# Normalising x in groups of 2, 2, 4 and 2 tiles, and comparing 100 of the 157 edge columns in the loop of head pairs

## What is computed

```python
xn = _layernorm(x, axis=-1)
x = x + gnn(xn, edge_index, W, b) + mix(xn)            # graph convolution, attention
x = x + ffn(_layernorm(x))                             # 8 experts, top 1, capacity 195
# gnn: deg = count of edges by target, msg = h[row] * norm, summed by target
# mix: 12 heads; A = q @ k.T; numerator = 1 + A + 0.5 * A * A; attn = numerator / its sum; attn @ v
```

## Time and profile before

| | us |
|---|---|
| median of 3 runs | 1186.23 (1185.6 to 1189.72) |
| the profiled execution | 1186.19 |
| its span in the trace | 1184.4 |
| PE, DVE, ACT, POOL busy | 943.1, 725.0, 471.5, 308.4 |

### The profile page before, as it was taken

One profiled execution on the slowest core, in us unless ns is written; L12 is line 12 of the kernel. 1 busy time (PEld: TensorE's weight loads), 2 busy tenths in 40 slices (PEclk: granted clock), 3 DMA queues, 4 the chain that ended last, 5 costly groups with the idle time before them and its releaser, 6 DMA issues.

```text
span 1184.4 us, 15348 instructions
## 1 busy us (share of the span) xinstructions
PE 943.1 (80%) x5388; PEld 901.2 (76%) x5388; DVE 725.0 (61%) x1357; ACT 471.5 (40%) x696; POOL 308.4 (26%) x204
## 2 busy tenths in 40 slices
PE   1138747999998998998999868979999975199970
PEld 1138746898898997997988758969999975099970
DVE  6248982677767768677778835564544437056633
ACT  1211012666676676676667721210110102156620
POOL 2013345566455554454520000000000001300004
PEclk9569988999999999999999988989999985599995
DMA  8986765222524324325215055365445113769987
GB/s 232 299 279 194 186 167 107 22 37 33 89 35 65 70 33 83 62 22 100 35 22 140 27 94 144 88 158 140 118 102 142 58 53 118 230 196 266 280 221 260
DMA packets 142147, 148.33 MB, mean 125 GB/s; under 512 B 71910, under 2 KB 119497, under 8 KB 140952
## 3 DMA queue, kind: packets, MB, share of 16 engines
q1 hardware_dynamic: 112152, 125.09, 39.6%
q0 software_dynamic: 29952, 22.68, 11.6%
HBM read 93.32 MB, written 46.72 MB: 118 GB/s over the span
## 4 chain that ended last, share of the span: by engine, by line
PE 55%; DVE 16%; DMA 10%; ACT 8%; issue 7%; SPq 2%; POOL 2%; DVEq 0%; ACTq 0%; POOLq 0%
PE ps L1635 12%; PE ps L1637 11%; PE ps L1636 11%; PE ps L1019 7%; DMA kb<-keyd 4%; DVE eqs L430 4%; PE ps L1003 4%; PE ps L1004 4%; ACT Pf L711 2%; ACT Ph L683 2%; DVE Pl L867 1%; DMA rows<-oE 1%; POOL rows L1376 1%; PE ps L1269 1%; PE ps L985 1%
## 5 line engine op out<-in xcount | busy, mean ns | idle before, releaser
L356 POOL DMA_INDIRECT counts<-countc,idxu x157 | 270.4, 1722 | 288.0 <-DMA counts<-countc,idxu 230.0
L867 DVE SCALAR_TENSOR_TENSOR Pl<-Pf,Ph 125x832 fp32r<-125x832 f32 (+1 forms) x180 | 184.6, 1027 | 117.9 <-ACT Ph L683 108.9
L711 ACT ACTIVATE Pf<-ps 125x832 f32<-125x832 f32 (+1 forms) x180 | 155.7, 866 | 116.4 <-PE ps L1004 108.1
L1019 PE MATMUL ps<-Ph,vsb 125*128 125x416 f32 (+1 forms) x360 | 129.0, 358 | 6.3 <-DVE Pl L867 6.1
L1019 PE MATMUL ps<-Pl,vsb 125*128 125x416 f32 (+1 forms) x360 | 126.6, 352 | 0.0
L1376 POOL DMA_INDIRECT rows<-XF,slots x10 | 14.8, 1483 | 397.5 <-DVE slots L1491 394.8
L1635 PE MATMUL ps<-wH,XH 128*125 128x384 f32 x240 | 85.4, 356 | 20.6 <-DVE VS L469 13.6
L1635 PE MATMUL ps<-XH,wqkH 128*128 128x416 f32 (+1 forms) x216 | 81.0, 375 | 20.5 <-DVE wqkL L758 12.1
L1636 PE MATMUL ps<-wL,XH 128*125 128x384 f32 x240 | 83.5, 348 | 0.0
L1637 PE MATMUL ps<-wH,XL 128*125 128x384 f32 x240 | 83.5, 348 | 0.0
L683 ACT ACTIVATE Ph<-Pf 125x832 fp32r<-125x832 f32 (+1 forms) x90 | 80.1, 897 | 0.7
(11 more groups left out here) (229 smaller groups left out, 2224.0 us busy)
## 6 DMA issues: line engine op xcount, KB each, us to landing
Cs<-counts SPq DMA_DIRECT2D x20, 546.9 KB
kb<-keyd SPq DMA_DIRECT2D x9, 1024.0 KB, 8.1
w1s<-L_ffn_w SPq DMA_DIRECT2D x8, 1152.0 KB, 8.2
w2s<-L_ffn_w SPq DMA_DIRECT2D x8, 1152.0 KB
odram<-OHL SPq DMA_DIRECT2D x12, 625.0 KB
oS<-odram SPq DMA_DIRECT2D x10, 750.0 KB, 4.8
vdram<-VS SPq DMA_DIRECT2D x10, 672.0 KB
vsb<-vdram SPq DMA_DIRECT2D x12, 560.0 KB
```

Source lines behind the costliest of these rows:

```text
L356: pool.indirect_dma_start(out=counts, out_offset=bass.IndirectOffsetOnAxis(ap=idxu[:, c:c + 1], axis=0), in_=countc[:, c:c + 1], in_offset ...
L711: act.activation(Pf[:, i % RING, :, 0:w], ps[0:T, 2 * (i % 2):2 * (i % 2) + 2, 0:w], ACT.Square, bias=1.0).then_inc(sq_done, 1)
L867: dve.scalar_tensor_tensor(out=p, in0=f, scalar=1.0, in1=h.bitcast(F32), op0=ALU.add, op1=ALU.subtract).then_inc(p_lo, 1)
L1019: ins = pe.matmul(ps[:, 4 + s % 2, 0:w], vsb[:, 2 * kp + t, a, :], part[:, m % RING, t, 0:w], start=(kp == 0 and t == 0 and part is Ph), s ...
```

## The change

x is normalised, transposed and split in four groups of 2, 2, 4 and 2 tiles, and value tiles 0, 1 and 2 stand between them on PE, ACT and DVE. The three parts of the value weights are loaded right behind the first two tiles of x, each with a buffer of its own (the third in the upper half of `kb`). The edge lists are loaded by ACT's queue. Only columns 0 to 55 and column 156 are compared in the value stage, in seven chunks of 8 behind value tiles 3 to 9, the lone one at the end. The other 100 are compared in the loop, 20 in each of the five pairs: SP loads their keys at the head of the pair into the memory of `kt2` (`kbp`), DVE waits for them at step 3, compares one column in each of steps 4 to 23, and works out the targets in steps 24 and 25. ACT waits for `eq_over` before it writes `kt2` again. POOL fills with zeros as soon as x and the three weights are there, and scatters 57 columns, then 20 for each pair.

The diff, cut to its core:

```diff
+EARLY = 56
+EG = 8
+EU = EARLY // EG
+EP = (ET - EARLY) // 5
+LONE = ET - 1
...
-        x_in = [sem(f"x_in{i}") for i in range(NT)]
+        x_in = [sem(f"x_in{i}") for i in range(NT // 2)]
...
+        kbp = kt2[:].rearrange("p t l f -> p (t l) f")
...
+        XGROUPS = [(0, 2), (2, 2), (4, 4), (8, 2)]
+        FIRST_EDGES = 3
+        def w_staging(wc):
+            return wst[:, wc, :, :] if wc < 2 else kb[:, 1, 0:12, :].rearrange("p s f -> p (s f)").rearrange("p (k n) -> p k n", k=2)
...
                 if i == 1:
-                    sp.wait_ge(padded, 1)
-                    for h, ends in enumerate((src, dst)):
...
+                    for wc in range(3):
+                        sp.dma_start(w_staging(wc), w_parts[0][0][2 * wc * P:2 * (wc + 1) * P, :].rearrange(
+                            "(k p) n -> p k n", p=P)).then_inc(w_early[wc], 16)
...
-            load_keys(0)
-            load_keys(1)
+            load_keys(0, 0, 0, EC)
+            sp.wait_ge(w_lo, 3)
+            load_keys(1, 0, EC, EC)
...
-                if i + 2 < EU:
-                    load_keys(i + 2)
+                if i == FIRST_EDGES + 1:
+                    sp.wait_ge(eq_done, 2)
+                    load_keys(0, 0, 2 * EC, EC)
+                if i == FIRST_EDGES + 3:
+                    sp.wait_ge(eq_done, 4)
+                    load_keys(1, 0, 3 * EC, EARLY - 3 * EC)
+                    load_keys(1, EARLY - 3 * EC, LONE, 1)
...
+            normalise(0)
+            split_w(0)
+            split_w(1)
+            turned_lo(0)
+            keys_of_edges()
+            split_w(2)
+            normalise(1)
+            value_lo(0)
+            turned_lo(1)
+            normalise(2)
+            value_lo(1)
+            turned_lo(2)
+            normalise(3)
+            value_lo(2)
+            turned_lo(3)
+            for i in range(3, NT):
+                value_lo(i)
+                edge_chunk(i - FIRST_EDGES)
...
+            def load_pair_keys(j):
+
+                sp.wait_ge(g_mm, j + 1)
+                sp.dma_start(kbp.bitcast(F32), keyd[at(j * EP + EARLY, EP), :].unsqueeze(0).broadcast_to([P, EP, P])
+                             ).then_inc(keys_in, 16)
...
             def turn(j, last):
+                if not last:
+                    load_pair_keys(j)
                 sp.wait_ge(oacc_done, 6 * j + FREE)
                 load_v(j, 1)
...
                         if i - 1 in TURN_AT:
+                            if i - 1 == TURN_AT[0]:
+                                act.wait_ge(eq_over, j + 1)
                             turn_k(j + 1, TURN_AT.index(i - 1))
...
                 for i in range(END):
 
+                    if not last:
+                        if i == PAIR_KEYS_AT:
+                            dve.wait_ge(keys_in, 16 * j + 16)
+                            dve.wait_ge(idx_ready, EU + j)
+                            order(dve.tensor_scalar(kcur[:], keyc[:, at(j * EP + EARLY, EP)], 1.0, None, ALU.mult))
+                        if PAIR_KEYS_AT < i <= PAIR_KEYS_AT + EP:
+                            pair_compare(i - PAIR_KEYS_AT - 1)
+                        if i in (PAIR_TARGETS_AT, PAIR_TARGETS_AT + 1):
+                            pair_targets(i - PAIR_TARGETS_AT)
```

More of the change, by code:

```diff
@@ new lines, in value_hi @@
+            def value_hi(i):
+                for c in range(2):
+                    vg = 2 * i + c
+                    act.wait_ge(v_mm, vg + 1)
+                    if i >= 2 and c == 0:
+                        act.wait_ge(v_store[i % 2], MOVED * (i // 2))
+                    act.activation(VS[:, i % 2, 6 * c:6 * c + 6, 0, :],
+                                   ps[0:T, 4 + vg % 4, 0:HALF].rearrange("p (h f) -> p h f", h=6), ACT.Copy
+                                   ).then_inc(v_hi, 1)
@@ L439, in edge_chunk, with targets @@
+            def targets(c0, n):
+                order(dve.tensor_scalar(etmp[:, 0, 0:n], countc[:, c0:c0 + n], AGAIN, None, ALU.is_ge))
+                for h in range(min(WINDOW, n)):
+                    order(dve.tensor_scalar(etmp[:, 1, h:n:WINDOW], keyc[:, c0 + h:c0 + n:WINDOW], -1.0,
                                             iota_f[:, 10 + h:11 + h], ALU.mult, ALU.add))
                 order(dve.tensor_tensor(etmp[:, 2, 0:n], etmp[:, 0, 0:n], etmp[:, 1, 0:n], ALU.mult))
-                ins = dve.tensor_tensor(idxu[:, cs], etmp[:, 2, 0:n], keyc[:, cs], ALU.add)
@@ L442, in edge_chunk @@
-                ins.then_inc(idx_ready, 1)
+                return dve.tensor_tensor(idxu[:, c0:c0 + n], etmp[:, 2, 0:n], keyc[:, c0:c0 + n], ALU.add)
+            def edge_chunk(u):
+                first, half = u * EG, (u // 2) % 2
+                if u % 2 == 0:
+                    dve.wait_ge(kb_in[half], (16 if u < EU - 1 else 32) + 16 * (u // 4))
+                for c in range(first, first + EG):
+                    ins = compare(c, half, c % EC, WINDOW)
+                    if c % 4 == 3:
+                        order(ins)
+                if u == EU - 1:
+                    order(compare(LONE, half, EARLY % EC, 1))
+                    order(targets(LONE, 1))
+                targets(first, EG).then_inc(idx_ready, 1)
@@ new lines, in value @@
+            def value(i):
+                for c in range(2):
+                    vg = 2 * i + c
+                    if vg >= 4:
+                        pe.wait_ge(v_lo, vg - 3)
+                    product(pe, ps[0:T, 4 + vg % 4, 0:HALF],
+                            lambda k: (XH[:, k, i * T:(i + 1) * T], XL[:, k, i * T:(i + 1) * T]),
+                            lambda k: (wH[:, k, c * HALF:(c + 1) * HALF], wL[:, k, c * HALF:(c + 1) * HALF]),
+                            KT).then_inc(v_mm, 1)
@@ new lines, in _ @@
+            turn_x(0)
+            pe.wait_ge(keys, 2)
+            pe.transpose(ps[:, 7, 0:P], keyA[:], ident[:])
+            pe.transpose(ps[:, 7, P:ET], keyB[:], ident[0:ET - P, 0:ET - P])
+            pe.wait_ge(b_in, 16)
+            ins = pe.transpose(ps[:, 7, ET:ET + 3 * PAIRS], brow[:], ident[0:3 * PAIRS, 0:3 * PAIRS])
+            ins.then_inc(key_tr, 1)
+            pe.wait_ge(keyc_done, 3)
+            pe.wait_ge(w_lo, 3)
+            pe.wait_ge(xt_lo, FIRST_UNIT[1])
+            value(0)
@@ L514, in build @@
+            turn_x(1)
+            pe.wait_ge(xt_lo, FIRST_UNIT[1])
+            value(1)
+            turn_x(2)
+            pe.wait_ge(xt_lo, FIRST_UNIT[2])
+            value(2)
+            turn_x(3)
+            pe.wait_ge(xt_lo, FIRST_UNIT[3])
+            value(3)
+            for i in range(4, NT):
+                if i == 8:
+                    pe.wait_ge(xt_lo, FIRST_UNIT[4])
+                value(i)
         HI_ON_ACT = [i % 5 in (1, 3) or i in (0, 27, 29) for i in range(STEPS)]
@@ L1381, in _ @@
             nodes_over(act)
[L1384 removed]
+            W1_BASE, W2_BASE = 48, 48
             def split_w1(e, b):
```

328 lines of the change are left out of this document (162 added, 166 removed).

## The result

The changed kernel takes **1226.57 us** (1225.16 to 1232.99, four runs) against 1186.64 for the kernel before on the same chip: a ratio of 1.0332 [1.0309, 1.0355]. It is slower by 39.9 us where 12 us less were forecast, and it lies above the range. The profiled execution is the slowest of the four (1232.99 us, span 1231.3); it is the only one with a trace. Behind the loop, where code and work are the same, it takes 498.4 us against 491.4 before; the other traces of this text that keep the loop's scatters as they are have 491.0 to 498.3 there, so these 7 us can't be laid to the change.

The account below looks back on a forecast made before the run. DVE bounds the value tiles; in the loop the chain lies on DVE and ACT at the head, then on PE. 1186.2 - 62 (value stage) + 49.6 (loop) = 1173.8 us, range 1161 to 1192 for 8 in 10.

Parts of the forecast that it names:

- The timeline of the value stage: Value stage: tile order and pace give the first read of K at 113.6 us before a margin for stores, gain 62.
- A store of VS has to land within about 8 us while zeros are being written, so I add 4: Value stage: allowance for stores beside zeros, 4 us added, putting the read of K at 118 (bounds 113 and 128).
- rival b: Value stage: DMA engines hold it, zeros starting with the stores; read of K at 128, gain 52, time 1183.8; chance 0.15.
- The wait at step 3: Loop, pairs 1 to 4: DVE waits 2.9 us until the keys' load is issued plus 6.5 for landing, 9.4 (7.9 to 13.0).
- the 13 that the prediction named as a sign of being wrong: Loop, step 3: forecast is wrong if DVE's idle time there is under 5 or over 13 us.
- The low clock: Loop, pairs 1 to 4: after a stop over 9 us PE runs about nine matmuls slower; 1.0 us taken (0 to 1.6).
- Comparisons from step 7 on at nothing: Loop: 17 comparisons and the targets lie in DVE's idle time beside PE's chain, cost nothing; without that cover 8.8 a pair.
- the 1.6 for the head alone: Loop, head of a pair: key copy and comparisons of steps 4 to 6 go straight in, 1.6 us.
- Pair 0, forecast at +1.6: Loop, first pair: keys land at about 208.5, before DVE reaches step 3 at 218.2; no wait, 1.6 us only.
- the forecast's 12.0: Loop, cost of each of pairs 1 to 4: 9.4 wait + 1.6 head + 1.0 clock = 12.0 us (9.5 to 16.2).
- The sixth pair: End of the loop: the sixth pair is unchanged, ending at about 682 us.
- The last scatter: POOL's scatters: their end moves from 604.5 to near 655 us, before the sixth pair ends, costing nothing.

## Why the prediction was wrong, step by step

**The timeline of the value stage: right.** Order, overlap and pace of the tiles were as worked out to 56 us, and with the rows' zeros out of the way the read of `K` comes at 114.6.

**"A store of VS has to land within about 8 us while zeros are being written, so I add 4": the step that failed.** The 8 us was what a store may take, and no row gave what it does take. For tiles 1 to 3 it takes 32 to 49 us. The prediction saw that zeros now start with the stores (rival b), but priced it by bytes: 106 us of DMA work in 108 us of time. Such a sum is a bound only if the engines always have work. Here the next store hangs on a tile that hangs on a store two tiles back, and from 76 to 110 us the engines are idle 38% of the time. Rival (b) named the right cause and priced it at 10 us (read of `K` at 128 in place of 118); it was 29.7. The run with the rows' zeros written later shows it, with the read of `K` at 114.6. By the counts above, a store beside these zeros got about one packet of 1 KB for each of 5 to 6 KB of zeros. This step makes 29.4 us of the 52.4 by which the sum is off.

**The wait at step 3: right in kind, 1.3 us short.** 2.9 + 6.5 was 9.4. It is 10.3 in pair 2 and 10.7 in the mean of pairs 2 to 4; of this 0.6 is the issue of the keys, 10.7 us behind the stores (378.07 against 367.36), where the next load came 10.1 behind them before. In the profiled run pair 1 has 15.2, beyond the 13 that the prediction named as a sign of being wrong. The fit of the Trainium skill (DMA: Bandwidth & Descriptors, Anatomy of one DMA), by which the load would take an estimated 5.0 us, is not borne out: the trace has 6.5.

**The low clock: 1.0 taken, a rest of 1.1 to 1.9 measured.** Between 386.3 and 391.2 twelve matmuls start about 0.35 us apart in place of 0.19, and between 393.9 and 399.7 some 14 more; the prediction reckoned nine, and took part of them as hidden. What the Trainium skill (TensorE: Matmul & The Clock Gate, HAM oscillation) says of a loop whose PE idles for DMAs, that it pays for the return each time, the traces bear out: with comparisons in the idle steps 0.93 to 0.95 in each pair with the wait, 1.00 in each without. The wait isn't the only cause of a low clock here: with no wait and one comparison in each step two pairs had 0.96 and 0.98.

**Comparisons from step 7 on at nothing: wrong.** They and those at the head cost 3.0 to 3.9 a pair against the 1.6 for the head alone; put three at a time into the idle steps, all of them cost 0.7. So their place costs, and not their number. My reading of why, from DVE's order and not from a run of its own: idle time of DVE ahead of a `Pl` covers only what stands in that step, so that one comparison in each step meets it in one step out of two or three, and in the others stands in front of a piece that PE wants. Pair 0, forecast at +1.6, fits in part: +4.2 with one a step, +1.0 with the idle steps and the wait and the copy `kcur` at step 8 (114.2 from the read of `K` to the pair's end). But with the idle steps and wait and copy at step 3 it is +3.1, and without comparisons in the loop still +2.6, though DVE stands for no keys in pair 0. So some 2 us of it go with the place of the wait and the copy, and why stays open.

**The rest: right.** The sixth pair is unchanged. The last scatter is at 701, not near 655, since the value stage and the pairs are longer, but it still ends before it is asked for.

With the two differences read from the trace, 1173.8 + 29.4 + 23 = 1226.2. Of the 23, 14.4 are the three terms above in four pairs: by the table a pair is 3.6 us dearer than the forecast's 12.0 (wait 1.2, clock 0.1 to 0.9, comparisons 1.4 to 2.3). Pair 0 adds 2.6. Some 6 belong to this one trace, 4.6 of them to the long wait in its pair 1.

## What to carry to other kernels

A stage that gets shorter pulls its transfers into the time of others: look for the longest landing that any row shows under that load (30.3 us here, behind a median of 8.1), and divide it by the buffers in flight, before a sum of bytes is trusted. A load that is put at the head of a turn of SP's queue starts when the stores of the last turn have landed; put it ahead of that wait, or let the engine that needs it come to it later. Spare time of an engine is worth what it is only in the steps where it stands.

## What the runs showed of the hardware

- A 750 KB store landed after 32 to 49 us (tiles 1 to 3) while another queue was writing zeros at the same time. That queue took 71.7% of the engines' time from 24 to 76 us, and 43.3% from 76 to 110.
- Stops of PE of 8.4 to 13.2 us (DVE's wait 10.3 to 15.2) and of 8.4 to 9.9 us (DVE's wait 6.0 to 7.7) brought the lower clock in every pair: 0.91 to 0.93 in the changed kernel, 0.94 to 0.96 with the wait at step 5. Behind the stop of 8.4 us in pair 2 some 26 matmuls started 0.35 us apart.
- Pairs of scatters to the same few spare cells landed after 8 to 19 us, and the stores of another queue beside them came late too (19 us from their issue to the next DMA, against 10.7).
- A comparison of 128x256 took 479 ns into bf16 and 481 into float32.
- Zeros asked for in pieces of 1 KB went in packets of 4,096 bytes, those in pieces of 3 KB in packets of 6,144: 752 or 880 more packets where 5,500 were expected.
- While stores in packets of 1,024 bytes and zeros in packets of 5,000 and 6,144 shared the engines, the two queues moved nearly as many packets, 761 and 776 in 20 us, and 0.75 against 4.52 MB.
